# A selective scan with an expert layer on one core: TensorE's slots reordered, routing of the first tokens made a chunk earlier

## The reference

```
x = x + scan_layer(layernorm(x))
x = x + expert_layer(layernorm(x))

scan_layer(x):                                    # D = 256, N = 16, rank 64
    B_t, C_t = x W_B^T, x W_C^T                   # 16 values a token each
    dt    = softplus((x W_dt1^T) W_dt2^T + b_dt2)
    A     = -exp(log_A)                           # 256 x 16
    A_bar = exp(dt * A)                           # per token, channel and n
    B_bar = (A_bar - 1) / (A + 1e-8) * x * B_t
    h_t   = A_bar * h_(t-1) + B_bar               # along a sequence
    y     = sum over n of h * C_t
    return y + D_skip * x

expert_layer(x):
    e = argmax(softmax(x Wr^T + br))              # one of 8 for each token
    return gelu(x W1[e] + b1[e]) W2[e] + b2[e]    # 256 -> 1024 -> 256
```

## Time and profile before

| | us |
|---|---|
| median of three runs | 820.6 (819.56 to 821.97) |
| profiled execution, its own time | 825.35 |
| its span in the trace | 823.6 |
| PE busy | 743.9 (90%) |
| DVE busy | 541.0 (66%) |
| POOL busy | 531.8 (65%) |
| ACT busy | 461.5 (56%) |

### The profile page before, as it was taken

The page is one execution under the profiler, slowest core; times in us unless marked ns, Lnnn a source line. Parts: engine busy times, 40 slices in busy tenths (PEclk is TensorE's granted clock), DMA queues, the critical chain, the costliest instruction groups (busy, mean ns, idle before and its releaser), DMA issues.

```text
span 823.6 us, 17041 instructions
## 1 busy us (share of the span) xinstructions
PE 743.9 (90%) x5514; PEld 688.0 (84%) x5515; DVE 541.0 (66%) x873; ACT 461.5 (56%) x943; POOL 531.8 (65%) x653
## 2 busy tenths in 40 slices
PE   3999999999999999979997968548999999999993
PEld 1888999899899999969897857437998999999992
DVE  7889989989989899898899843412333333333320
ACT  3868898888888978767676635111333332333320
POOL 2799989988899899769999633352333333433330
PEclk9899999999999999998998989778999999999997
DMA  8676642323332333124479482111111111111100
GB/s 283 199 259 231 221 142 99 119 83 104 130 104 92 130 103 130 64 78 110 80 79 91 134 312 59 31 18 55 51 49 46 41 42 52 48 41 52 35 9 0
DMA packets 44374, 82.47 MB, mean 100 GB/s; under 512 B 6280, under 2 KB 14733, under 8 KB 44304
## 3 DMA queue, kind: packets, MB, share of 16 engines
q1 hardware_dynamic: 38288, 68.98, 29.7%
q0 software_dynamic: 6016, 12.61, 5.2%
HBM read 70.41 MB, written 13.91 MB: 102 GB/s over the span
## 4 chain that ended last, share of the span: by engine, by line
PE 63%; DMA 7%; issue 6%; DVE 5%; POOL 4%; ACT 4%; POOLq 0%; DVEq 0%; ACTq 0%
PE WW L908 18%; PE misc L1006 15%; PE WW L990 14%; PE YY L926 8%; DMA y_out<-CbX,gcol 5%; DVE w_sb L1087 2%; ACT w_sb L733 2%; ACT Csb L722 2%; POOL lists L574 2%; DMA mag<-token_rows,gcol 1%; POOL w_sb L568 1%; PE misc L861 1%; PE misc L846 1%; PE misc L836 1%; PE misc L872 1%
## 5 line engine op out<-in xcount | busy, mean ns | idle before, releaser
L568 POOL TENSOR_TENSOR w_sb<-w_sb,Csb 128x512 f32<-128x512 f32 x182 | 231.7, 1275 | 45.2 <-DVE w_sb L1087 29.4
L803 ACT ACTIVATE dt<-WW,b1c 128x128 f32<-128x128 f32 x312 | 88.7, 369 | 225.7 <-PE WW L990 225.7
L908 PE MATMUL WW<-b_sb,xin 128*128 128x129 f32 (+1 forms) x1536 | 207.5, 285 | 8.0 <-DVE w_sb L1107 6.0
L908 PEld LDWEIGHTS WW<-b_sb,xin 128*128 128x128 f32 x1536 | 191.5, 198 | 22.8 <-issue 11.1
L1087 DVE TENSOR_TENSOR_SCAN w_sb<-WW,hlast,w_sb 128x512 f32<-128x512 f32 x138 | 173.0, 1270 | 15.2 <-PE WW L908 15.2
L733 ACT ACTIVATE w_sb<-dt,negA 128x512 f32<-128x512 f32 x256 | 170.6, 710 | 11.5 <-DVE w_sb L1087 10.2
L1006 PE MATMUL misc<-w_sb,dt 128*128 x624 | 148.4, 393 | 2.7 <-ACT dt L803 1.5
L1006 PEld LDWEIGHTS misc<-w_sb,dt 128*128 128x128 f32 x624 | 120.6, 198 | 20.5 <-issue 4.4
L926 PE MATMUL YY<-sm,w_sb 128*128 128x128 f32 x1024 | 126.8, 273 | 2.3 <-POOL w_sb L568 2.3
L990 PE MATMUL WW<-z,xin 128*128 128x128 f32 x624 | 122.1, 278 | 0.1
L926 PEld LDWEIGHTS YY<-sm,w_sb 128*128 128x128 f32 x1024 | 114.7, 141 | 2.5 <-POOL w_sb L568 2.5
(11 more groups left out here) (207 smaller groups left out, 907.1 us busy)
## 6 DMA issues: line engine op xcount, KB each, us to landing
w_sb<-c_rows SPq DMA_DIRECT2D x86, 256.0 KB
CbX<-c_rows SPq DMA_DIRECT2D x42, 256.0 KB
w_sb<-w_in SPq DMA_DIRECT2D x20, 512.0 KB, 6.0
token_rows<-row SPq DMA_DIRECT2D x8, 1024.0 KB
w_sb<-w_in SPq DMA_DIRECT2D x24, 256.0 KB
xin<-x_in SPq DMA_DIRECT2D x8, 512.0 KB, 4.1
w_sb<-x_in SPq DMA_DIRECT2D x7, 512.0 KB, 8.7
b_sb<-b_in SPq DMA_DIRECT2D x1, 774.0 KB, 4.6
```

The lines of the kernel that those rows point to most:

```text
L568: eng.tensor_tensor(hc[g % NHC], hb_of(g), Csb[i % NCS][:, :], ALU.mult).then_inc(s_hcp, 1)
L803: g = eng.activation(hT[u % 2][:, j * P:(j + 1) * P], hps[u % 2][:, j * P:(j + 1) * P], ACT.Gelu, bias=b1c[u][:, j:j + 1])
L908: mm = eng.matmul(bank_of_w[:, i * P:i * P + width], x_rows[:, i, h * P:(h + 1) * P], bands[m % NR][:, i, 0:width], start=(i == 0), stop=( ...
```

## The change

Six things, all in one edit.

1. **Order of a slot.** On TensorE every slot is y, y, w, w, shared product.
2. **VECTOR_N.** Chunk 5 gets n = 3 more, chunk 6 loses n = 13.
3. **Batch 0 a chunk earlier.** The product rank goes to slot 0 of chunk 5. choose(0) is cut into four parts at the end of chunk 4, place_tokens(0) into two at item 3 of chunk 5, first_table into five at the end of chunk 6 (from item 14 of chunk 7). Its 16 enlists go to every second slot from n = 5 of chunk 5 on, the last two to chunk 7. Lists, keep_ids, the gathers of tiles 0 to 2 and the turn of tiles 0 and 1 move forward within chunk 7, choose(1) is cut into four parts.
4. **ocol.** VectorE copies the token numbers for the put into a buffer of their own, after waiting for the put of four tiles before; gather(t) waits only until finish(t - 4) is done.
5. **Start.** TensorE multiplies ones and zeros (80 + 24 matmuls) before its first inputs are there; VectorE normalizes two of the first four row tiles; dt2_0 comes before brow, vlast behind the first four w.
6. **softmax_exp** of ScalarE moves from slot 1 of the chunk after next to slot 14 of the next one (13 in the last).

```diff
-VECTOR_N = [(1, 3, 5, 8, 11, 13)] + [(1, 5, 8, 11)] * 5 + [(1, 3, 5, 8, 11, 13), (1, 4, 7, 10, 13)]
+VECTOR_N = [(1, 3, 5, 8, 11, 13)] + [(1, 5, 8, 11)] * 4 + [(1, 3, 5, 8, 11)] * 2 + [(1, 4, 7, 10, 13)]
-FIRST = ("xn0", "xn1", "bcd", "brow", "dt2_0", "dt2_1", "vlast")
+FIRST = ("xn0", "xn1", "bcd", "dt2_0", "brow", "dt2_1", "vlast")
 def hops(q):
-        if q == 6:
-            at |= {0: ("rank", 3)}
+        if q == BATCHES[0][1] + 1:
+            at |= {0: ("rank", BATCHES[0][1] - 1)}
     else:
-        at = {1: ("cbt", q), 3: ("u01", q), 4: ("u23", q), 7: ("xnr0", q - 1), 8: ("xnr1", q - 1), 9: ("route", q - 1),
-              11: ("lists", 0), 15: ("rank", 6)}
+        at = {1: ("cbt", q), 3: ("u01", q), 4: ("u23", q), 6: ("lists", 0), 8: ("xnr0", q - 1), 9: ("xnr1", q - 1),
+              10: ("route", q - 1), 13: ("turn", 0), 15: ("rank", 6)}
...
-                    if q == NQ - 2 and 4 <= n < 14:
-                        enlist(0, (n - 4,))
-                    if last and n < 6:
-                        enlist(0, (n + 10,))
-                    if last and n > 12:
-                        gather(n - 13, n - 13, 0)
-                        b1_copy(n - 13, n - 13)
+                    if q == NQ - 3 and n > 4 and n % 2:
+                        enlist(0, ((n - 5) // 2,))
+                    if q == NQ - 2 and n % 2:
+                        enlist(0, ((n + 11) // 2,))
+                    if last and n < 2:
+                        enlist(0, (n + 14,))
+                    if last and 8 <= n < 11:
+                        gather(n - 8, n - 8, 0)
+                        b1_copy(n - 8, n - 8)
...
             def gather(t, u, r):
-                wait(eng, s_out[u], 16 * r)
+                wait(eng, s_yo, t - 3)
                 eng.tensor_copy(gcol[u][:, :], ids[:, bass.ds(c, 1)]).then_inc(s_gcol, 1)
...
             def put(t, u):
-                    out=outrows, out_offset=bass.IndirectOffsetOnAxis(ap=gcol[u][:, :], axis=0),
+                    out=outrows, out_offset=bass.IndirectOffsetOnAxis(ap=ocol[u][:, :], axis=0),
...
                 if name == "u01" and q == NQ - 1:
+                    eng.wait_ge(s_first, 1)
...
             def emit(q):
                 for n in range(N):
                     m = N * q + n
-                    if n < 2 or n in VECTOR_N[q]:
-                        add_y(KD * m - 4)
-                        add_y(KD * m - 3)
-                        if n in at:
-                            fill(*at[n])
-                        make_w(KD * m + 4)
-                        make_w(KD * m + 5)
-                    else:
-                        make_w(KD * m + 4)
-                        if n in at:
-                            fill(*at[n])
-                        make_w(KD * m + 5)
-                        add_y(KD * m - 4)
-                        add_y(KD * m - 3)
+                    add_y(KD * m - 4)
+                    add_y(KD * m - 3)
+                    make_w(KD * m + 4)
+                    make_w(KD * m + 5)
+                    if n in at:
+                        fill(*at[n])
+
+            eng.wait_ge(s_pconst, 6)
+            for i in range(80):
+                eng.matmul(bank[1][:, 0:P], ones_bf[:, :], ones_bf[:, :], start=True, stop=True)
+            for i in range(24):
+                r = 64 * (i % 2)
+                eng.matmul(bank[i % 2][:, 0:BAND], zeros[r:r + 64, 0:P], zeros[r:r + 64, 0:BAND], start=True, stop=True)
...
             aggregate(0, 0)
+            eng.wait_ge(s_rs[0], 1)
+            for i in range(2):
+                ins = eng.tensor_scalar(xin[0][:, i, :], xin[0][:, i, :], rs[0][:, i:i + 1], nm[0][:, i:i + 1], ALU.mult,
+                                        ALU.add)
...
-                    if (j, gap) in (((10, 1), (12, 1)) if last else ((28, 1), (30, 1))):
-                        u_times_x(q, j // (12 if last else 30))
-                    if q == 5 and (j, gap) == (29, 1):
-                        choose(0, ("u01", 5))
-                    if q == 6 and (j, gap) == (3, 0):
-                        place_tokens(0)
-                    if last and (j, gap) == (14, 1):
-                        first_table()
+                    if (j, gap) in (((9, 1), (11, 1)) if last else ((28, 1), (30, 1))):
+                        u_times_x(q, j // (11 if last else 30))
+                    if q == BATCHES[0][1] and (j, gap) in ((29, 0), (29, 1), (30, 0), (31, 0)):
+                        choose(0, 2 * j + gap - 58 - int(j == 31))
+                    if q == BATCHES[0][1] + 1 and j == 3:
+                        place_tokens(0, (gap,))
+                    if q == NQ - 2 and (j, gap) in ((29, 0), (29, 1), (30, 0), (31, 0), (31, 1)):
+                        first_table(2 * j + gap - 58 - int(j == 31))
...
             def finish(t, u, r):
                 e = eng.value_load(tile_eu[0:1, bass.ds(t, 1)], min_val=0, max_val=E - 1)
+                wait(eng, s_out[u], 16 * r)
+                eng.tensor_copy(ocol[u][:, :], gcol[u][:, :])
                 eng.wait_ge(s_yp, t + 1)
-                wait(eng, s_out[u], 16 * r)
```

More of the change, by code:

```diff
@@ L266, in build @@
         gcol = [sb(f"gcol{i}", [P, 1], U32) for i in range(4)]
+        ocol = [sb(f"ocol{i}", [P, 1], U32) for i in range(4)]
         cum = col("tri", 0, E + 1)
@@ L271, in build @@
         red = col("tri", 32, 33)
+        zeros = tail[:, 0:BAND]
         big = tail[:, 0:TC]
@@ L760, in emit @@
                         norm2(q - 1, (2 * (n - 6), 2 * (n - 6) + 1))
-                    if q > 1 and n == 1:
-                        softmax_exp(q - 2)
-                    if last and n == 12:
+                    if not first and n == (13 if last else 14):
                         softmax_exp(q - 1)
@@ L770, in _ @@
             eng.wait_ge(s_rs[0], 1)
-            norm1(0, range(TI), rs[0], nm[0])
+            norm1(0, (2, 3), rs[0], nm[0])
             for name in FIRST:
@@ L827, in fill @@
                     eng.wait_ge(s_z, 2 * NQ)
+                if name == "u01" and q == NQ - 1:
+                    eng.wait_ge(s_first, 1)
                 if name in ("xn0", "xn1"):
                     h = int(name[-1])
+                    if q == 0:
+                        eng.wait_ge(s_xnv, 1)
                     eng.wait_ge(s_xn, q + 1)
@@ L960, in _ @@
                 make_w(g)
+            fill(FIRST[-1], 0)
             for q in range(NQ):
                 emit(q)
-            fill("turn", 0)
             def turn_x(t, u, r):
@@ L1163, in logits, with choose @@
                    .then_inc(s_lg, 1)
-            def choose(batch, before):
+            def choose(batch, part):
                 q0, q1 = BATCHES[batch]
@@ L1176, in over_e, with place_tokens @@
                     return ap.unsqueeze(2).to_broadcast([P, tiles, E])
-                wait_read(eng, *before)
-                eng.wait_ge(s_pe, q1)
-                done(eng.tensor_reduce(top, mine, AX.X, ALU.add), "rt")
-                done(eng.reciprocal(top, top), "rt")
-                done(eng.tensor_tensor(mine, mine, over_e(top), ALU.mult), "rt")
-                done(eng.tensor_reduce(top, mine, AX.X, ALU.max), "rt")
-                done(eng.tensor_tensor(found, mine, over_e(top), ALU.is_equal), "rt")
-                done(eng.tensor_tensor(found, found, less8, ALU.mult), "rt")
-                done(eng.tensor_reduce(top, found, AX.X, ALU.min), "rt")
-                eng.tensor_tensor(onehot[:, 0:tiles, :], over_e(top), less8, ALU.is_equal).then_inc(s_oh, 1)
-            def place_tokens(batch):
+                if part == 0:
+                    wait_read(eng, *(("u01", q1), ("u01", q1), ("route", NQ - 1))[batch])
+                    eng.wait_ge(s_pe, q1)
+                    done(eng.tensor_reduce(top, mine, AX.X, ALU.add), "rt")
+                    done(eng.reciprocal(top, top), "rt")
+                elif part == 1:
+                    done(eng.tensor_tensor(mine, mine, over_e(top), ALU.mult), "rt")
+                    done(eng.tensor_reduce(top, mine, AX.X, ALU.max), "rt")
+                elif part == 2:
+                    done(eng.tensor_tensor(found, mine, over_e(top), ALU.is_equal), "rt")
+                    done(eng.tensor_tensor(found, found, less8, ALU.mult), "rt")
+                else:
+                    done(eng.tensor_reduce(top, found, AX.X, ALU.min), "rt")
+                    eng.tensor_tensor(onehot[:, 0:tiles, :], over_e(top), less8, ALU.is_equal).then_inc(s_oh, 1)
+            def place_tokens(batch, parts=(0, 1)):
                 q0, q1 = BATCHES[batch]
@@ L1197, in place_tokens @@
                 before = col("e_base").unsqueeze(2) if batch == 0 else run[batch - 1][:, :, (q0 - BATCHES[batch - 1][0]) * TI:(q0 - BATCHES[batch - 1][0]) * TI + 1]
[L1198 to L1204 removed]
+                if 0 in parts:
+                    eng.wait_ge(s_full, HOP["rank", q1 - 1] + 1)
+                    keep = z[1][:, 256:256 + E * (tiles + 1)]
+                    done(eng.memset(keep, 1.0), "rt")
```

(9 more changed lines are left out.)

92 lines of the change are left out of this document (49 added, 43 removed).

## The result

| | before | changed |
|---|---|---|
| median (5 runs each) | 820.6 (817.3 to 822.0) | 828.1 (826.8 to 831.4) |
| ratio | | 1.0109 (1.0076 to 1.0143) |
| profiled execution, its span | 825.35, 823.6 | 828.11, 826.4 |

In the four later sets of runs, on four chips, the kernel before had medians of 821.9 to 824.9. The profiled execution of before lay 4.75 above its median, that of the changed kernel on it: by the traces the change costs 2.8 us, by the medians 7.5.

What follows compares the result with a forecast made beforehand. TensorE bounds the scan phase, waits the expert phase's start; a TensorE-VectorE round is hidden by 0.4 us. Start +0.6, scan +21.2, chunk 7 -6.6, expert phase -25 and -1: -10.8 on 820.6, put at 810 (785 to 829).

Steps and rivals of the forecast that it cites:

- the round: Scan phase: u01 releases VectorE, whose item 11 releases w 15 of the next chunk; from 53.8 to 57.45 us.
- the floor of chunk 7: Last scan chunk: VectorE's busy 53.0 less 3.0 gives 50.0 us, so -6.6, between 0 and -8.
- The order of a slot: TensorE's slots in the scan phase: bcd and u01 now come last, making each round 3.2 us longer than 54.2.
- The first stretch: From w 15 (slot 5) to the end of u01 (slot 13), TensorE without pause: 26.56 us becomes 30.04.
- The second stretch: From the end of u01 to the end of VectorE's item 11 in the next chunk: 27.2 us becomes 27.4.
- That puts u23 about 4.2 us after u01: In the second stretch u23 stands behind w 33, 4.2 us after u01 instead of 3.9: +0.2.
- T: The end of the last w item, from which the expert phase is counted; 471.4 in the kernel before.
- The expert phase: From T: outputs(0) at T + 19.5, turn(6) at T + 61 against 86.3, -25 (best -35, worst -6); later -1.
- The change is the same on both: The profiled execution's -10.8 us was applied unchanged to the median 820.6, giving 809.8.
- The hidden round: Scan phase: the round stays hidden, so the part to chunk 7 gains 4 us, not loses 21; 785; chance 0.18.
- The clock rival: Chunks 1 to 6: waits bring one half-clock spell each, 3.4 us apiece, +20 in all; 830 us; chance 0.17.
- The third rival: Expert phase gives back only 8 to 12 us, gathers 4 to 6 and w2 landing behind enlists; 824 to 828; chance 0.13.

Runs made afterwards that it cites:

- 3: Changed kernel with u01 alone moved to the head of slot 13 (chunks 0 to 6): 831.9 us, ratio 1.0086.
- 2: The kernel before with only the new slot order: 849.7 us, ratio 1.0323.
- 8: Changed kernel with the slot order of before and the gather of tile 2 moved to slot 15 of the last chunk: 804.6 us, ratio 0.9778.
- 1: Changed kernel with the slot order of before, all else as changed: 816.1 us, ratio 0.9899.
- 10: Changed kernel with the slot order and start of before and the gather of tile 2 at slot 15: 807.1 us, ratio 0.9828.
- 5: Changed kernel with the gather of tile 2 moved from slot 10 to slot 15 of the last chunk: 828.9 us, ratio 1.0090.
- 14: Changed kernel without the 16 enlists of batches 1 and 2, so fewer rows in later tiles: 821.1 us, ratio 0.9981.

## Why the prediction was wrong

The forecast was 810, with 785 to 829 held; 828.1 is inside the range and on the other side of before.

By its own test (chunks 1 to 3 within 1 us of 57.4) it failed in chunks 1 and 2, at 58.95 and 58.92, and held in chunk 3, at 58.07. Two steps failed: the size of the round, by 6.6 us, and the floor of chunk 7, by 6.7. Without these two errors the sum would stand at 5.8 us less than before, in place of 7.5 more.

**The order of a slot** was the right mechanism with the right sign, and too small. The step "The round is 30.04 + 27.4 = 57.45 us" measured 58.1 to 58.95. The first stretch lacked 0.5 to 0.8: the w items of slots 8 and 11, which follow VectorE's products, take 2.55 and 2.15 us in chunk 1 and 2.28 and 2.07 in chunk 3, where the other pairs take 1.95; the longest wait for VectorE is 0.33 us. I had taken TensorE to run through it ("Nothing in it can be made shorter by VectorE"). The second stretch was right in chunk 3 (27.2) and 0.6 short in chunk 1. "That puts u23 about 4.2 us after u01" measured 4.37; what I missed is that u23 is a second contact, and moving u01 alone gives nothing (3). Chunk 0 lost 3.85, not 2.1. The order alone costs it 3.3 (57.0 in 2, 53.7 before), so 1.2 are missing in the sum of the order; the new start, of which I had expected nothing after the first scan, costs 1.0 to 2.0 with the old order (8 and 1 against 10) and 0.5 here. Chunk 4 lost 5.1: the order alone costs it 4.0 (2), the rest of the change, with choose(0) now at its end, 1.6 (1); chunks 5 and 6 together 5.9 against a forecast 6.3. In all this is 6.6 us of the error.

**Chunk 7** failed outright: -6.6 forecast, +0.1 measured. I took out the first table and the half clock and did not count what moves in: three gathers of 2.3 us on GpSimd, whose products ScalarE, and then VectorE, wait for. "VectorE's busy 53.0 less 3.0 gives the floor, 50.0" was a floor of one engine, 48.4 busy of 56.6 measured. The third gather is worth 3.1 us of it (5) and the slot order 1.2 (1); with both undone (8) the chunk takes 52.4 up to T, 4.3 less than before. The last 2.3 of the 6.6 stay open: no run moved the other two gathers or the parts of choose(1).

**The expert phase** came near, partly by luck. From T (499.7): hidden(0) at T + 4.5, outputs(0) at T + 22.0 (19.5 forecast: its wait for the upper part of w2 did not shrink, as the last of those transfers was issued at T + 11.5, where I had T + 8, and landed at T + 20.1), turn(6) at T + 64.6 (61). No wait for y_out:

```profile
529.89 1.00 POOL L634 DMA_INDIRECT y_out<-CbX,ocol  x1 [7.45 <-DVE CbX L1410]
...
530.85 0.23 POOL L620 COPY gcol<-ids 128x1 uint32 x1
...
541.20 1.07 POOL L622 DMA_INDIRECT mag<-token_rows,gcol  x1 [0.86 <-POOL gcol L620]
...
555.36 1.07 POOL L622 DMA_INDIRECT mag<-token_rows,gcol  x1 [0.86 <-POOL gcol L620]
```

Turn 4 was free, turns 5 and 6 idle 2.3 us each, and outputs(0), (3) and (4) ran wholly or partly at half clock after such waits, with a granted clock of 0.58, 0.57 and 0.74 in 6.3, 6.5 and 5.0 us, where the others take 3.6 at 1.00. Before, three of them did so too (outputs 2, 3 and 4: 6.4, 5.3 and 6.4 us at 0.57, 0.70 and 0.57):

```profile
521.68 6.28 PE L1016 MATMUL misc<-w_sb,dt 128*128 x16 [8.14 <-issue]
...
551.11 0.69 PE L981 MATMUL YY<-sm,mag 128*128 128x128 f32 x2 [2.29 <-DMA mag<-token_rows,gcol]
...
551.97 6.49 PE L1016 MATMUL misc<-w_sb,dt 128*128 x16 [0.18 <-issue]
...
564.35 0.65 PE L981 MATMUL YY<-sm,mag 128*128 128x128 f32 x2 [2.31 <-DMA mag<-token_rows,gcol]
```

The gather of tile 5 landed 9.9 us after its issue at 541.20 with enlists ahead and around it, that of tile 6 8.9; the median is 3.4. By the Trainium skill's rule (DMA: Bandwidth & Descriptors, "Queues, rings and completion order") a gather's semaphore lands behind every earlier write of its DMA engine. The trace agrees: the put issued at 538.62 landed at 549.98, and the gather issued behind it at 551.06. 14, where the enlists are gone and both turns are free, shows that the enlists are what both wait behind; whether by this rule or by the time that the enlists take on the DMA engines, the runs do not tell. I had let only the gather of tile 6 land late, by 11.8, from T + 48; it was issued at T + 55.7, 7.7 later, and landed sooner, and the gather of tile 5 was late as well. That the stretch came within 3.5 us of the forecast is luck in part. Of these 3.5 us of the error 2.5 are there at outputs(0); 2.9 others came back after turn(6).

**From the span to the median.** "The change is the same on both" cost 4.7 us: the profiled execution of before was a long one of its kernel, and that of the changed kernel was not. The later medians of before (821.9 to 824.9) lie nearer to the profiled one.

**The rivals.** The hidden round did not come. The clock rival named the right side for the wrong reason: chunks 1 to 4 and 6 ran at 1.00, chunk 5 at 0.95, and chunks 0 and 7 at 0.97. In chunks 1 to 4 the waits of 1.2 us before the first y did not bring the clock down. The third rival's 824 to 828 is next to where the time came out, but its reason, only 8 to 12 us given back in the expert phase, is not what happened: 21.5 were, and 25.4 with what follows turn(6).

## What to carry to other kernels

Two engines that are each over 90% busy (here 54.0 and 49.7 of 54.2 us) are tied by rounds across their queues; before an order is changed, cut the trace at the contacts and add up each round, through every product that the other engine waits for, not the nearest only. A round that had 0.4 us of slack turned 3.5 us of reordering that looked harmless into up to 4.5 us a chunk. Where work is moved into a stretch, count it on each engine's queue there: what leaves is seldom the only thing that changes. And take a change apart: here one part (ocol) was worth -17 to -19 us (-14 on before alone), one (the slot order) +25 to +26.5, and their sum looked like 1%.
